# Graph-attention layer, one core: SyncE alone waits for the final stores, and shares the last block's first stores with GpSimd

## Chip, cores and metric

The kernel runs on one core of one Trainium2 chip. The metric is the device time of one execution in microseconds (us), lower is better. The kernel before takes 256.71 us, the median of 3 runs (256.52 to 256.77).

## What is computed

A graph-attention layer, then a residual and a layer norm, for N = 4096 nodes with D = 128 features. `adj` is a 4096 x 4096 matrix of int32 zeros and ones.

```python
s_i = emb @ attn[:d]
s_j = emb @ attn[d:]
e = leaky_relu(s_i + s_j.T, negative_slope=0.2)
e = e + where(adj > 0, 0.0, -1e9)
alpha = softmax(e, axis=1)
x = layernorm(x + alpha @ emb)
```

## The kernel before

The program is written engine by engine, and each engine runs its own list in the order in which it is written; semaphores are set by hand. SyncE (SP) and ScalarE (ACT) issue the loads: each takes one half of the partitions, in quadrants of 32 (`LOW_HALF` is quadrants 0 and 1 for SP, `HIGH_HALF` quadrants 2 and 3 for ACT). The matrix `adj` comes in 32 pieces, 8 blocks of 512 output rows with 4 pieces each. ScalarE makes mask bytes of a piece, VectorE (DVE) turns them and builds the weights (L721), and TensorE (PE) multiplies weights by features and sums in PSUM (L866, and L870 for the last block, where the four output tiles are summed one after the other).

Seven blocks are normalised by ScalarE and GpSimd (POOL) while the next block is computed, and GpSimd stores each with four DMAs (L346, semaphore `stored`). The last block of four tiles is finished in three groups, `FINAL_GROUPS`: tiles 0 and 1, then tile 2, then tile 3. `EARLY` is 1, so the first group is the early one:

- the early group (tiles 0 and 1): GpSimd computes scale and offset (L351 to L358), ScalarE applies them (L503) and raises `early_out_ready`, and GpSimd stores the group with four DMAs, one a quadrant, 32 KB each, whose completion counts on `early_stored`;
- the other two groups: VectorE normalises them (L698) and raises `last_out_ready`; SP stores quadrants 0 and 1, ACT quadrants 2 and 3, 16 KB each, two DMAs a group and engine, counted on `last_stored`.

All of these stores are issued by the one helper `store_last`, so each of them has line 279:

```python
queue.dma_start(out_v[f, q, :, k * D:(k + n) * D],
                x_raw[B * q:B * (q + 1), FINAL + v.start:FINAL + v.stop, :].rearrange("b k d -> b (k d)")
                ).then_inc(done, 16)
```

After its stores SP reads a flag, `again` (L306), that says whether a slow path for extreme inputs has to run; ACT, DVE and PE read it too (L526, L762, L911). With these inputs no engine takes that path. Then SP waits for `last_stored` (L316), which counts the stores of ACT too, and GpSimd waits for `early_stored` (L363). ACT waits for `stored` before it reads the flag (L522). At the end of the program's block (L91) each engine has a branch, a DRAIN and an event-semaphore instruction; GpSimd, which has two of these, gathers the arrivals of the others and then releases them. No engine leaves the block before all have come to its end. The waits on `last_stored` and `early_stored` are attached to the branches of L91.

Of the kernel before, what the change touches and what calls it, by code (L numbers as in the profile page):

```python
# [13 lines left out]
def gat_kernel(nc: bass.Bass, x: bass.AP, adj: bass.AP, attn: bass.AP, out: bass.AP):  # L14
# [11 lines left out]
    Q = 4  # L26
# [9 lines left out]
    LOW_HALF = (0, 1)  # L36
    HIGH_HALF = (2, 3)
# [23 lines left out]
    FINAL_GROUPS = [slice(0, 2), slice(2, 3), slice(3, 4)]  # L61
    EARLY = len(FINAL_GROUPS) - 2
# [28 lines left out]
    with ExitStack() as ctx:  # L91
# [3 lines left out]
        def sem(name):  # L95
            return ctx.enter_context(nc.semaphore(name))
# [111 lines left out]
        early_out_ready = sem("early_out_ready")  # L208
        last_out_ready = sem("last_out_ready")
        early_stored = sem("early_stored")  # L210
        last_stored = sem("last_stored")
# [37 lines left out]
        def load_x(queue, quadrants, part):  # L249

            first, stop = X_CUTS[part], X_CUTS[part + 1]
            for q in quadrants:
                queue.dma_start(x_raw[B * q:B * (q + 1), first:stop, :].rearrange("b (f k) d -> b f (k d)", k=K),  # L253
                                x_v[q, :, first // K:stop // K, :]).then_inc(x_loaded[part], 16)

        def load_piece(queue, quadrants, g):

            if g >= IN_FLIGHT:
                landed = g - IN_FLIGHT
                queue.wait_ge(adj_loaded[landed % ADJ_SLOTS], 16 * Q * (landed // ADJ_SLOTS + 1))  # L260
            if g == PROD_SLOT:
                queue.wait_ge(row_max_ready, 1)
            elif g == XT_SLOT:
                queue.wait_ge(s_i_in_psum, RB)
            elif ADJ_SLOTS <= g < ADJ_SLOTS + BY_DVE:
                queue.wait_ge(half_bytes_ready, 1)
                queue.wait_ge(first_bytes_ready, g - ADJ_SLOTS + 1)
            elif g >= ADJ_SLOTS + BY_DVE:
                queue.wait_ge(bytes_ready, g - ADJ_SLOTS - BY_DVE + 1)
            for q in quadrants:  # L270
                queue.dma_start(adj_in[B * q:B * (q + 1), g % ADJ_SLOTS, :, :, :],  # L271
                                adj_v[g // PIECES, g % PIECES, q, :, :, :, :]).then_inc(adj_loaded[g % ADJ_SLOTS], 16)

        def store_last(queue, g, q, done):

            v = FINAL_GROUPS[g]
            f, k = (FINAL + v.start) // K, v.start % K
            n = v.stop - v.start
# [3 lines that stand above are left out]
# [7 lines left out]
        @block.sync  # L289
        def _(sp):  # L290

            sp.dma_start(attn_row_in[:], attn[:, :].rearrange("d o -> o d")).then_inc(attn_loaded, 16)  # L292
            for part in range(X_PARTS):
                load_x(sp, LOW_HALF, part)
            for g in range(ALL_PIECES):
                load_piece(sp, LOW_HALF, g)


            for g in range(EARLY, len(FINAL_GROUPS)):
                sp.wait_ge(last_out_ready, g - EARLY + 1)  # L300
                for q in LOW_HALF:
                    store_last(sp, g, q, last_stored)


            sp.wait_ge(again_ready, 1)
            with sp.If(sp.value_load(again[0:1, 0:1], min_val=0, max_val=1) > 0):  # L306
                sp.wait_ge(stored, 16 * Q * NORM_GROUPS)
                sp.wait_ge(early_stored, 16 * Q * EARLY)
                sp.wait_ge(last_stored, 16 * Q * (len(FINAL_GROUPS) - EARLY))
                sp.dma_start(xi[:], xi_v).then_inc(inputs_again, 16)  # L310
                sp.dma_start(attn_col, attn[D:2 * D, :]).then_inc(inputs_again, 16)
                sp.dma_start(attn_row, attn[0:D, :].rearrange("d o -> o d").broadcast_to([P, D])).then_inc(inputs_again, 16)
                with sp.Fori(0, TILES) as t:
                    sp.wait_ge(adj_rows_free, t + 1)
                    sp.dma_start(adj_rows, adj[bass.ds(t * P, P), :]).then_inc(adj_rows_loaded, 16)
            sp.wait_ge(last_stored, 16 * Q * (len(FINAL_GROUPS) - EARLY))  # L316

        @block.gpsimd
        def _(pool):
            nc.gpsimd.memset(ident[:], 0.0).then_inc(ident_zeroed, 1)  # L320
            pool.wait_ge(ident_zeroed, 1)
            nc.gpsimd.affine_select(out=ident[:], in_=ident[:], compare_op=ALU.not_equal, fill=1.0, base=0,
                                    pattern=[[-1, P]], channel_multiplier=1).then_inc(consts_ready, 1)
            nc.gpsimd.memset(half[:], -0.5)
            nc.gpsimd.memset(eps[:], EPS)
            nc.gpsimd.memset(rden[:], 0.0)
            nc.gpsimd.memset(worst[:], 0.0).then_inc(worst_ready, 1)
            pool.wait_ge(products_ready, STRIPES)
            nc.gpsimd.tensor_scalar(neg_last[:], x_raw[:, :, DEN], -1.0, 0.0, ALU.mult, ALU.add).then_inc(neg_last_ready, 1)
            pool.wait_ge(neg_last_ready, 1)  # L330
            pool.wait_ge(factors_ready, 1)
            nc.gpsimd.tensor_tensor(last_x[:], neg_last[:], d_j[:], ALU.mult).then_inc(last_x_ready, 1)

            for g in range(NORM_GROUPS):

                pool.wait_ge(total_ready, g + 1)
                nc.gpsimd.tensor_scalar(neg_mean[:, 0:K], total[:, 0:K], -1.0 / D, 0.0, ALU.mult, ALU.add).then_inc(mean_ready, 1)  # L337
                pool.wait_ge(squares_ready, g + 1)
                nc.gpsimd.tensor_scalar(variance[:, 0:K], square_sum[:, 0:K], 1.0 / D, EPS, ALU.mult, ALU.add).then_inc(variance_ready, 1)
                pool.wait_ge(variance_ready, g + 1)  # L340
                nc.gpsimd.tensor_tensor(rstd[:, 0:K], variance[:, 0:K], half[:, 0:K], ALU.pow).then_inc(rstd_ready, 1)  # L341
                pool.wait_ge(rstd_ready, g + 1)
                nc.gpsimd.tensor_tensor(offset[:, 0:K], neg_mean[:, 0:K], rstd[:, 0:K], ALU.mult).then_inc(offset_ready, 1)  # L343
                pool.wait_ge(out_ready, g + 1)
                for q in range(Q):
                    pool.dma_start(out_v[g, q, :, :],  # L346
                                   x_raw[B * q:B * (q + 1), g * K:(g + 1) * K, :].rearrange("b k d -> b (k d)")).then_inc(stored, 16)

            for g, v in enumerate(FINAL_GROUPS[:EARLY]):
                pool.wait_ge(moments_ready, v.stop)  # L350
                nc.gpsimd.tensor_scalar(variance[:, v], moments[:, v, 1], 1.0, EPS,  # L351
                                        ALU.mult, ALU.add)
                nc.gpsimd.tensor_scalar(neg_mean[:, v], moments[:, v, 0], -1.0, 0.0,
                                        ALU.mult, ALU.add).then_inc(variance_ready, 1)
                pool.wait_ge(variance_ready, NORM_GROUPS + g + 1)
                nc.gpsimd.tensor_tensor(rstd[:, v], variance[:, v], half[:, v], ALU.pow).then_inc(rstd_ready, 1)
                pool.wait_ge(rstd_ready, NORM_GROUPS + g + 1)
                nc.gpsimd.tensor_tensor(offset[:, v], neg_mean[:, v], rstd[:, v], ALU.mult).then_inc(offset_ready, 1)  # L358
            for g in range(EARLY):
                pool.wait_ge(early_out_ready, g + 1)  # L360
                for q in range(Q):
                    store_last(pool, g, q, early_stored)
            pool.wait_ge(early_stored, 16 * Q * EARLY)  # L363

        @block.scalar
        def _(act):
# [608 lines left out]
```

## Time and profile before

| what | value |
|---|---|
| median of 3 runs (lowest to highest) | 256.71 us (256.52 to 256.77) |
| the profiled execution's own time | 257.18 us |
| its span, first to last instruction | 255.3 us |
| PE busy | 242.9 us, 95% of the span |
| DVE busy | 233.6 us, 91% |
| ACT busy | 175.4 us, 69% |
| POOL busy | 36.5 us, 14% |
| DMA traffic | 71.51 MB |

Times in the rows are us from the span's start unless marked ns. "Busy" counts work instructions alone; branches, drains, semaphore instructions and the issuing of DMAs by SP and ACT are not in it, and are found under the line that holds them, with a q behind the engine's name (POOLq is GpSimd's sequencer). "DMA to landing" runs from the start of an issue to the moment at which its data have landed.

### The profile page before, as it was taken

The page shows a single profiled execution, that of the slowest core. Times are in us where ns is not written, and L with a number is a line of the kernel's source. Part 1 is how long each engine was busy: PE and PEld are TensorE (multiplying, and loading weights), DVE is VectorE, ACT ScalarE, POOL GpSimd, SP SyncE. Part 2 cuts the span into 40 slices and gives each one's busy share as a digit, 9 for nine tenths or more (in the row PEclk, how much of TensorE's full clock was granted, in tenths as well). Part 3 has the DMA queues.
Part 4 walks back from the last instruction along what each step waited for, and adds up shares of the span by engine and source line. Part 5 has one row for each costly group of instructions (what it writes and reads, how often), then busy time and mean ns, then how long its engine had stood idle before and what let it go on. Part 6 is the DMA issues. An engine that isn't in the chain of part 4 may idle for free.

```text
span 255.3 us, 2776 instructions
## 1 busy us (share of the span) xinstructions
PE 242.9 (95%) x801; PEld 127.9 (50%) x801; DVE 233.6 (91%) x383; ACT 175.4 (69%) x257; POOL 36.5 (14%) x76
## 2 busy tenths in 40 slices
PE   7998989989999999999999999999999999999980
PEld 6743434434444444444444444444444444899970
DVE  1979899989999999999999999999999999999552
ACT  0589999998499669495986579578965579204410
POOL 1000000000052003300430003300320004303322
PEclk9999999999999999999999999999999999999997
DMA  7999999999999999999999999999999940100101
GB/s 199 309 347 348 348 349 347 349 342 348 347 328 360 349 348 348 348 335 348 348 347 364 347 348 348 353 349 348 349 360 350 346 116 0 45 0 4 41 0 45
DMA packets 70227, 71.51 MB, mean 280 GB/s; under 512 B 2881, under 2 KB 68674, under 8 KB 70210
## 3 DMA queue, kind: packets, MB, share of 16 engines
q10 hardware_dynamic: 34592, 34.67, 43.5%
q1 hardware_dynamic: 34594, 34.67, 43.4%
q0 software_dynamic: 1024, 1.97, 2.5%
q8 instruction: 7, 0.11, 0.2%
q14 instruction: 10, 0.08, 0.1%
HBM read 69.21 MB, written 2.10 MB: 279 GB/s over the span
## 4 chain that ended last, share of the span: by engine, by line
PE 81%; ACT 6%; DMA 5%; issue 2%; ACTq 2%; SPq 1%; POOL 1%; DVE 1%
PE psum L866 69%; PE psum L870 11%; DMA adj_in<-in_adj_dram 5%; ACT xj L400 2%; ACTq L271 2%; ACT mask_bytes L412 2%; ACT mask_bytes L418 1%; PE psum L862 1%; SPq L253 1%; POOL out_dram L279 1%; ACT x_raw L503 0%; SPq L271 0%; DVE weights L721 0%; DVE x_raw L666 0%; SPq L292 0%
## 5 line engine op out<-in xcount | busy, mean ns | idle before, releaser
L866 PE MATMUL psum<-weights,xj 128*128 128x512 f32 x448 | 194.5, 593 | 2.9 <-ACT xj L400 2.0
L721 DVE SCALAR_TENSOR_TENSOR weights<-q_row,r_j,mask_t 128x512 f32<-128x512 f32 x256 | 172.2, 740 | 0.3
L866 PEld LDWEIGHTS psum<-weights,xj 128*128 128x128 f32 x448 | 84.0, 190 | 109.2 <-issue 82.2
L418 ACT ACTIVATE mask_bytes<-adj_in 128x4096 uint8<-128x4096 int32 x27 | 97.3, 3613 | 22.7 <-DMA adj_in<-in_adj_dram 15.2
L607 DVE STREAM_TRANSPOSE mask_t<-mask_bytes 128x1024 uint32<-128x1024 uint32 x27 | 33.4, 1236 | 0.9 <-ACT mask_bytes L418 0.9
L870 PEld LDWEIGHTS psum<-xj,weights 128*128 128x128 f32 x256 | 28.8, 192 | 0.5 <-issue 0.5
L870 PE MATMUL psum<-xj,weights 128*128 128x128 f32 x256 | 28.9, 275 | 0.0
L337 POOL TENSOR_SCALAR neg_mean<-total 128x4 f32<-128x4 f32 x7 | 1.6, 223 | 158.4 <-ACT x_raw L431 158.4
L431 ACT ACTIVATE x_raw<-x_raw 128x128 f32<-128x128 f32 x28 | 8.2, 295 | 15.3 <-DVE x_raw L666 15.3
L346 POOL DMA_DIRECT2D out_dram<-x_raw x28 | 14.6, 525 | 19.3 <-ACT x_raw L445 19.3
L412 ACT ACTIVATE mask_bytes<-adj_in 128x2048 uint8<-128x2048 int32 x9 | 17.0, 1901 | 0.0
L400 ACT ACTIVATE xj<-x_raw,last_x,d_j 128x127 f32<-128x127 f32 x32 | 13.2, 485 | 1.2 <-issue 1.2
L445 ACT ACTIVATE x_raw<-x_raw,offset,rstd 128x128 f32<-128x128 f32 x28 | 11.5, 480 | 2.6 <-POOL offset L343 2.6
L438 ACT ACTIVATE unused<-x_raw,neg_mean 128x128 f32<-128x128 f32 x28 | 10.9, 390 | 2.5 <-POOL neg_mean L337 2.5
L426 ACT COPY sums<-psum 128x512 f32<-128x512 f32 x7 | 4.1, 585 | 12.2 <-PE psum L866 12.2
L341 POOL TENSOR_TENSOR rstd<-variance,half 128x4 f32<-128x4 f32 x7 | 9.9, 1419 | 0.6
L666 DVE SCALAR_TENSOR_TENSOR x_raw<-psum,rden,x_raw 128x127 f32<-128x127 f32 x32 | 9.2, 343 | 0.4
L620 DVE STREAM_TRANSPOSE mask_t<-mask_bytes 128x512 uint32<-128x512 uint32 x10 | 7.1, 708 | 1.8 <-ACT mask_bytes L412 1.6
L833 PE MATMUL psum<-adj_in,attn_iw 128*128 128x512 f32 x16 | 7.6, 598 | 0.0
L511 ACT ACTIVATE deviations<-moments,eps 128x1 f32<-128x1 f32 x2 | 0.6, 294 | 8.5 <-DVE moments L690 8.5
L654 DVE TENSOR_SCALAR rden<-psum 128x4 f32<-128x4 f32 (+2 forms) x10 | 1.5, 154 | 5.3 <-PE psum L870 5.3
L822 PE MATMUL psum<-ident,x_raw 128*128 128x128 f32 x32 | 6.0, 350 | 0.3 <-DMA x_raw<-in_x_dram 0.3
(65 smaller groups left out, 81.7 us busy)
## 6 DMA issues: line engine op xcount, KB each, us to landing
adj_in<-in_adj_dram ACTq DMA_DIRECT2D x64, 512.0 KB, 13.0
adj_in<-in_adj_dram SPq DMA_DIRECT2D x64, 512.0 KB, 13.6
out_dram<-x_raw POOLq DMA_DIRECT2D x28, 64.0 KB, 5.3
x_raw<-in_x_dram ACTq DMA_DIRECT2D x4, 128.0 KB, 3.2
x_raw<-in_x_dram SPq DMA_DIRECT2D x4, 128.0 KB, 3.5
x_raw<-in_x_dram ACTq DMA_DIRECT2D x2, 256.0 KB, 6.1
x_raw<-in_x_dram SPq DMA_DIRECT2D x2, 256.0 KB, 7.0
out_dram<-x_raw POOLq DMA_DIRECT2D x4, 32.0 KB, 1.8
```

The lines of the kernel that those rows point to most:

```text
L341: nc.gpsimd.tensor_tensor(rstd[:, 0:K], variance[:, 0:K], half[:, 0:K], ALU.pow).then_inc(rstd_ready, 1)
L346: pool.dma_start(out_v[g, q, :, :], x_raw[B * q:B * (q + 1), g * K:(g + 1) * K, :].rearrange("b k d -> b (k d)")).then_inc(stored, 16)
L400: nc.scalar.activation(xj[:, c, 0:DEN], x_raw[:, c, 0:DEN], ACT.Identity, bias=last_x[:, c:c + 1], scale=d_j[:, c:c + 1]).then_inc(xj_scal ...
L412: half_bytes = nc.scalar.activation(mask_bytes[:, g % BYTE_SLOTS, :, :, part], adj_in[:, g % ADJ_SLOTS, :, :, part], ACT.Sign)
L418: nc.scalar.activation(mask_bytes[:, g % BYTE_SLOTS, :, :, :], adj_in[:, g % ADJ_SLOTS, :, :, :], ACT.Sign).then_inc(bytes_ready, 1)
L438: last = nc.scalar.activation(unused[:, k, :], tile(g * K + k), ACT.Square, bias=neg_mean[:, k:k + 1], accum_out=square_sum[:, k:k + 1])
L445: last = nc.scalar.activation(tile(g * K + k), tile(g * K + k), ACT.Identity, bias=offset[:, k:k + 1], scale=rstd[:, k:k + 1])
L607: nc.vector.transpose(dst.rearrange("p f (r a) -> p r f a", a=B), src).then_inc(mask_ready, 1)
L666: nc.vector.scalar_tensor_tensor(features, sums_of(n, t)[:, 0:DEN], rden[:, t:t + 1], features, ALU.mult, ALU.add).then_inc(y_ready, 1)
L721: nc.vector.scalar_tensor_tensor(weights[:, slot_of(n, c), :], q_row[:, n * BANK:(n + 1) * BANK], r_j[:, c:c + 1], mask_t[:, (n * PIECES + ...
L866: nc.tensor.matmul(banks[SUM_BANK[n % 2]][:, :], xj[:, c, :], weights[:, slot_of(n, c), :], start=(c == 0), stop=(c == CHUNKS - 1)).then_i ...
L870: return nc.tensor.matmul(banks[((BLOCKS - 1) * K + t) % 8][:, 0:D], weights[:, slot_of(BLOCKS - 1, c), t * P:(t + 1) * P], xj[:, c, :], s ...
```

## The change

SP issues quadrants 0 and 1 of the early group, ahead of its other four stores, and counts them on `last_stored`. GpSimd issues quadrants 2 and 3 of it, still on `early_stored`, and no longer waits for them; SP waits for both semaphores at the end. The counts in the waits are adapted. The slow path's waits change with them and are not executed.

```diff
@@ sync (SP)
+            for g in range(EARLY):
+                sp.wait_ge(early_out_ready, g + 1)
+                for q in LOW_HALF:
+                    store_last(sp, g, q, last_stored)
             for g in range(EARLY, len(FINAL_GROUPS)):
                 sp.wait_ge(last_out_ready, g - EARLY + 1)
                 for q in LOW_HALF:
...
                 sp.wait_ge(stored, 16 * Q * NORM_GROUPS)
-                sp.wait_ge(early_stored, 16 * Q * EARLY)
-                sp.wait_ge(last_stored, 16 * Q * (len(FINAL_GROUPS) - EARLY))
+                sp.wait_ge(early_stored, 16 * len(HIGH_HALF) * EARLY)
+                sp.wait_ge(last_stored, 16 * (Q * len(FINAL_GROUPS) - len(HIGH_HALF) * EARLY))
...
-            sp.wait_ge(last_stored, 16 * Q * (len(FINAL_GROUPS) - EARLY))
+            sp.wait_ge(early_stored, 16 * len(HIGH_HALF) * EARLY)
+            sp.wait_ge(last_stored, 16 * (Q * len(FINAL_GROUPS) - len(HIGH_HALF) * EARLY))
 
         @block.gpsimd
...
             for g in range(EARLY):
                 pool.wait_ge(early_out_ready, g + 1)
-                for q in range(Q):
+                for q in HIGH_HALF:
                     store_last(pool, g, q, early_stored)
-            pool.wait_ge(early_stored, 16 * Q * EARLY)
```

On GpSimd the end of the list reads so before (a row is a line, an operation, its output and input, and in brackets the semaphores that it waits for):

```order
L358 TENSOR_TENSOR offset<-neg_mean,rstd 128x2 [waits rstd_ready]
L279 DMA out_dram<-x_raw 32x256 [waits early_out_ready]
L279 DMA out_dram<-x_raw 32x256 x3
L91 UNCONDITIONAL_BRANCH [waits early_stored]
```

and so after the change (its line 363 is line 358 of before):

```order
L363 TENSOR_TENSOR offset<-neg_mean,rstd 128x2 [waits rstd_ready]
L279 DMA out_dram<-x_raw 32x256 [waits early_out_ready]
L279 DMA out_dram<-x_raw 32x256
L91 UNCONDITIONAL_BRANCH
```

Two of four DMA issues are gone from GpSimd, and the branch to the block's end waits for nothing. On SP, between its last loads of `adj` and the reading of the flag, the difference is:

```order
 L271 DMA adj_in<-in_adj_dram 32x16x256
+L279 DMA out_dram<-x_raw 32x256 [waits early_out_ready]
+L279 DMA out_dram<-x_raw 32x256
 L279 DMA out_dram<-x_raw 32x128 [waits last_out_ready]
 L279 DMA out_dram<-x_raw 32x128
 L279 DMA out_dram<-x_raw 32x128 [waits last_out_ready]
 L279 DMA out_dram<-x_raw 32x128
```

The two stores of the early group stand ahead of SP's four others. The branch of L91 on SP now waits for two semaphores:

```order
-L91 UNCONDITIONAL_BRANCH [waits last_stored]
...
+L91 UNCONDITIONAL_BRANCH [waits last_stored,early_stored]
```

Nothing moves on PE, DVE and ACT.

## Rows read from the trace of the kernel before

**Rows 1.** The page: the span, and busy time by engine.
```profile
span 255.3 us, 2776 instructions
PE 242.9 (95%) x801; PEld 127.9 (50%) x801; DVE 233.6 (91%) x383; ACT 175.4 (69%) x257; POOL 36.5 (14%) x76
```

**Rows 2.** End of the chain that ended last: start us, us, what.
```profile
225.38 20.56 PE psum L870 x184
...
247.64 0.78 ACT x_raw L503 x2
248.42 0.28 issue
248.70 0.59 POOL out_dram L279
249.29 0.00 issue
249.29 1.47 POOL out_dram L279 x3
```

**Rows 3.** The block's end, L91, on all engines: ns min/median/max, first and last start us.
```profile
L91 POOLq EVENT_SEMAPHORE  x2: 17/17/17, 255.1 to 255.2; - x2
L91 DVEq DRAIN  x1: 17/17/17, 251.7 to 251.7; - x1
L91 PEldq DRAIN  x1: 73/73/73, 251.9 to 251.9; - x1
L91 POOLq COMPARE_BRANCH  x1: 33/33/33, 252.3 to 252.3; - x1
L91 POOLq DRAIN  x1: 2674/2674/2674, 252.4 to 252.4; - x1
L91 ACTq DRAIN  x1: 81/81/81, 252.7 to 252.7; - x1
L91 SPq COMPARE_BRANCH  x1: 38/38/38, 253.1 to 253.1; - x1
L91 SPq DRAIN  x1: 7/7/7, 253.2 to 253.2; - x1
```

**Rows 4.** What SP's queue waited for, 247 to 256 us: total, times, longest.
```profile
SPq L91 <- PEq L91: 2.0, 1, 2.0
SPq L91 <- DMA out_dram<-x_raw: 0.9, 1, 0.9
```

**Rows 5.** The program's start, L965: GpSimd's DRAIN.
```profile
L965 POOLq DRAIN  x1: 169/169/169, 0.3 to 0.3; - x1
```

**Rows 6.** GpSimd's stores of the early group (L279), the first two, then the last two.
```profile
L279 POOL DMA_DIRECT2D out_dram<-x_raw x2: 496/544/593, 248.7 to 249.3; - x2
DMA to landing us min/median/max: 1.8/1.8/1.8
L279 POOL DMA_DIRECT2D out_dram<-x_raw x2: 496/498/501, 249.8 to 250.3; - x2
DMA to landing us min/median/max: 1.9/1.9/2.0
```

**Rows 7.** The last two stores of SP, and of ACT (L279).
```profile
L279 SPq DMA_DIRECT2D out_dram<-x_raw x2: 423/428/432, 250.3 to 250.8; - x2
DMA to landing us min/median/max: 1.9/2.0/2.0
L279 ACTq DMA_DIRECT2D out_dram<-x_raw x2: 438/440/443, 250.4 to 250.9; - x2
DMA to landing us min/median/max: 2.1/2.2/2.2
```

**Rows 8.** Timeline from 248 us: start us, us, engine, line, instructions.
```profile
249.12 0.34 DVE L698 TENSOR_SCALAR x_raw<-x_raw,moments,rstd 128x128 f32<-128x128 f32 x1
249.49 1.75 SPq L279 DMA_DIRECT2D out_dram<-x_raw  x4
249.49 1.81 ACTq L279 DMA_DIRECT2D out_dram<-x_raw  x4
```

**Rows 9.** Issues on SP: other loads, and the branch of the flag (L306).
```profile
L253 SPq DMA_DIRECT2D x_raw<-in_x_dram x6: 353/427/432, 1.1 to 3.4; - x6
L271 SPq DMA_DIRECT2D adj_in<-in_adj_dram x64: 579/2816/6242, 3.9 to 193.4; - x64
L306 SPq COMPARE_BRANCH  x1: 50/50/50, 252.1 to 252.1; - x1
```

**Rows 10.** Instruction queues by DMA window: 252 to 252.7, then 253.1 to 253.6.
```profile
q8 instruction: 1, 0.02, 11.5%
q14 instruction: 1, 0.01, 5.7%
```

## Prediction
> **What bounds the kernel now.** I read the page first: TensorE is busy for 95% of the span [rows 1]. The change touches none of its work, so all that it can win or lose lies behind the last product. The second view is the chain of waits [rows 2]. TensorE's sum of tile 2 ends at 245.94, ScalarE finishes the early group at 248.42, and then the chain runs over GpSimd's four store issues, 248.70 to 250.76. There it stops, 4.5 us before the span ends at 255.3, because the rest is sequencer instructions that are not counted as work. So the third view is the block's end, L91, engine by engine [rows 3]. In order of arrival: VectorE drains at 251.7, TensorE at 251.9, ScalarE at 252.7, SP at 253.2. GpSimd branches at 252.3, starts its DRAIN at 252.4 and is in it for 2674 ns, until 255.04. Its two event-semaphore instructions (gather, release) follow at 255.1 and 255.2, and the span ends at 255.3, 0.26 us behind the drain's end. Every other engine has stood ready since 253.2: SP waited 2.0 us for the release, after 0.9 us for the last store to land [rows 4]. The row names TensorE as releaser, but TensorE had arrived at 251.9; the release comes from GpSimd. **The end of the kernel is GpSimd's DRAIN, and that starts where the last of GpSimd's four stores has landed.** The landing that the wait of L363 waits for: the last issue starts at 250.27 and lands 2.0 us later, 252.27 [rows 6], and the branch goes at 252.3.
>
> **The change, part by part.**
>
> Removed: GpSimd's wait. The branch then follows the last issue at once instead of at its landing. With four issues that would be 250.77 instead of 252.3, so 1.5 us.
>
> Removed: two of GpSimd's issues, the last two, 496 to 501 ns each [rows 6], so 1.0 us more. GpSimd's issues then end at 249.29 + 0.50 = 249.79. The step from its release to the start of the drain was 0.1 us (252.3 to 252.4), so the drain starts at about 249.9, 2.5 us earlier.
>
> The drain's length with two stores in flight is shown by no row, since both drains of the trace find the queue empty. The bounds are 169 ns, the drain of the start, before GpSimd has stored anything [rows 5], and 2674 ns plus all the time until its stores have landed. I take 2674 ns flat: it is the one drain at the same place behind the same kind of DMA. Then it ends at 249.9 + 2.67 = 252.6. With 169 ns it would end at 250.1; for the span the two are the same, since both lie before SP's 253.2. GpSimd's gather is then complete only when SP arrives.
>
> Added on SP: two issues in front of its four. Its queue has been idle since the loads. `early_out_ready` comes at 248.42; SP follows a release by 0.03 us (VectorE ends at 249.46, SP issues at 249.49 [rows 8]). Two issues at the 0.43 us of SP's later stores [rows 7] end at 249.31, which is 0.18 us before the moment at which SP has its next work, so they cost nothing. The cover is thin: SP's issues of the larger loads of `x` take 353 to 432 ns, but those of `adj` at least 579 ns [rows 9]. With 579 ns the two end at 249.61 and all that SP has behind them slips by 0.12 us. Who waits for SP? Only the block's end.
>
> Moved wait: SP waits for `early_stored` as well. GpSimd's second issue starts at 249.29 and lands 1.8 us later, at 251.1 [rows 6]; SP's own two, issued before 249.0, land by about 251. SP itself reaches its branch of the flag at 252.1 [rows 9] and then waits for ACT's last store, which is issued at 251.30 - 0.44 = 250.86 and lands 2.2 us later, at 253.06 [rows 7, 8]. So the new wait ends 2 us before the old one: free. If SP's stores slip by 0.12 us, its last one lands at 250.81 + 0.12 + 2.0 = 252.9, still before ACT's.
>
> Traffic: before, the last two GpSimd stores (249.8 to 252.3) flew beside the 16 KB stores of SP and ACT; now that data leaves earlier. ACT's last two stores took 2.1 and 2.2 us, SP's 1.9 and 2.0, GpSimd's first 1.8 [rows 6, 7]. At best ACT's last takes 1.8 and lands at 252.7, 0.4 us earlier; at worst nothing changes. I take nothing, and keep the 0.4 for the range.
>
> **The sum.** SP's drain is over at 253.2, as before. A step of about 0.1 us from SP's arrival to GpSimd, which until now had no place on the path (my estimate, from the 0.1 us between landing and branch and between branch and drain in rows 3), then the 0.26 us of gather and release: the span ends at 253.55 instead of 255.3, so 1.75 us less. The profiled execution takes 257.18 us by its own clock, 0.47 over the median of the runs; its 1.88 us outside the span I leave as they are. 257.18 - 1.75 = 255.43 for a profiled execution, and against the runs 256.71 - 1.75 = **255.0 us**. What is late next is ACT's last store. Removing the wait alone would have given a drain end of 250.77 + 0.1 + 2.67 = 253.54 and a gain of 1.5 us; the moved stores are thus worth some 0.25 us, as they bring the drain's end below SP's arrival.
>
> **The rivals.**
>
> *The drain waits for GpSimd's own stores (A').* If stores in flight count as GpSimd's work, the drain cannot be done before they land at 251.1. If its 2.67 us then begin, it ends at 251.1 + 0.1 + 2.67 = 253.9, the span at 254.15, 1.15 us less: 255.6 us. For it: the 2.67 us stand behind DMAs while the drain of the start took 0.17. Against it: 2.67 us were needed although everything had landed, so the time is no waiting for data. The Trainium skill's "PSUM — Partial Sum Buffer", section "Engine vs sequencer instructions", says that a drain waits for the engine to go fully idle; it does not say whether a transfer in flight counts as activity. By that rule, read strictly, the result is this rival's; no row before shows it.
>
> *The instruction queues.* One block of instructions is fetched between 252 and 252.7, another between 253.1 and 253.6 [rows 10], while everybody stands in the barrier. If an engine needs one of them to leave, a release at 253.4 comes too early, and the end (in the span or behind it) is at about 253.9 instead of 253.55: 255.4 us. For it: the fetch begins behind the end of all work. Against it: at 255.3 the engines left within 0.1 us, which says only that the block was there by then.
>
> *The change does not do what it says.* The drain might end by something that the change leaves alone, for example 1.95 us behind the landing of the last store of any engine (253.06 + 1.98 = 255.04). Then it only gets longer by as much as it starts earlier, 5.1 us, and the time stays at 256.7. For it: only one long drain is seen, so its start may be coincidence. Against it: the other engines' drains beside stores in flight or just landed took 7 and 81 ns [rows 3].
>
> *Slower: the drain pays for each open store.* If the drain, in addition to its 2.67 us, works 2.67 us on every store that it finds open, it takes 3 x 2.67 = 8.0 us from 249.9, ends at 257.9, and the span at 258.2: 2.9 us more, 259.6 us. It decides from a drain of 5.1 us on (249.9 + 5.1 = 255.04); above 5.7 us the loss could be measured. For it speaks that the change starts a drain with open stores for the first time; against it, that the drain before had 32 stores behind it and took 2.67 us in all, 84 ns for each.
>
> **How the numbers follow.** My forecast, the flat drain off the path: 0.55, at 255.0, by itself 254.6 (ACT's landing 0.4 earlier) to 255.2 (SP's slip and the 0.13 us by which the runs scatter). Instruction fetch: 0.12, at 255.4. Drain behind the landing: 0.18, at 255.6. No effect: 0.10, at 256.7. Slower: 0.05, at 259.6. A measurement of this kernel can tell 0.2%, 0.5 us, from no change. The first three cases all lie more than that below 256.71, so faster is 0.85, the same 0.10, slower 0.05. The range has to take in the first three; from 254.5, a tenth below the forecast's own low end, to 256.0, a third of a microsecond above the drain behind the landing, for a drain that is a little longer there. Left out are the 0.15 of the last two cases.
>
> **What would show it.** Right: in the rows of the block's end GpSimd's branch stands at 249.8 and its DRAIN starts at 249.9 and ends before 253; SP's DRAIN stays at 253.2 and the span ends within 0.4 us of it; SP's queue no longer waits 2 us for a release; SP's six stores are issued without a gap that moves the last one past 250.8. The drain's length tells the cases apart: 2.67 us or less is mine, 4.0 is the drain behind the landing, 5.1 the unchanged end, more than 5.7 the loss. A span of 253.9 with a drain that ended at 252.6 speaks for the instruction queues. The prediction is wrong if the drain still ends last, or if ACT's last store lands later than 253.1.

## Result: 2.3 us faster, more than forecast

The changed kernel takes **254.08 us**, the median of 4 runs (253.61 to 254.91), against 256.74 us for 4 runs of the kernel before (256.52 to 256.91). The ratio is 0.991, 95% interval 0.9891 to 0.9928, so it is faster by 1.8 to 2.8 us, 2.3 us by the ratio; the two medians themselves lie 2.66 us apart. The forecast was 255.0 us in a range of 254.5 to 256.0: the direction is right, the time lies below the range.

The profiled execution of the changed kernel took 254.91 us, of which the span is 253.0. Its page, for [rows 1]:

```profile
span 253.0 us, 2776 instructions
PE 243.4 (96%) x801; PEld 128.1 (51%) x801; DVE 233.6 (92%) x383; ACT 175.5 (69%) x257; POOL 36.4 (14%) x74
```

TensorE's and VectorE's work is the same to 0.5 us; GpSimd has two instructions fewer. The block's end, for [rows 3], with L310 in place of L306 for SP's branch of the flag:

```profile
L91 POOLq EVENT_SEMAPHORE  x2: 17/17/17, 252.8 to 252.9; - x2
L91 POOLq DRAIN  x1: 3249/3249/3249, 249.0 to 249.0; - x1
...
L91 SPq COMPARE_BRANCH  x1: 38/38/38, 252.6 to 252.6; - x1
L91 ACTq DRAIN  x1: 81/81/81, 252.6 to 252.6; - x1
L91 SPq DRAIN  x1: 7/7/7, 252.8 to 252.8; - x1
...
L310 SPq COMPARE_BRANCH  x1: 50/50/50, 252.1 to 252.1; - x1
```

GpSimd's DRAIN is now recorded from 249.0 on, while its first store is still being issued (the second follows from 249.2 to 249.7), and is over at 252.3. SP arrives at 252.8 and is the last; 0.2 us later the span ends. The waits of SP's queue, for [rows 4] (L321 is the wait for `last_stored`):

```profile
SPq L321 <- DMA out_dram<-x_raw: 0.3, 1, 0.3
...
SPq L91 <- PEq L91: 0.2, 1, 0.2
```

The 2.0 us in which SP stood at the barrier are 0.2. The timeline, for [rows 8], and the last two stores of SP and ACT with their landing, for [rows 7]:

```profile
247.46 0.86 ACT L507 ACTIVATE x_raw<-x_raw,offset,rstd 128x128 f32<-128x128 f32 x2
248.35 2.87 SPq L279 DMA_DIRECT2D out_dram<-x_raw  x6
248.62 1.09 POOL L279 DMA_DIRECT2D out_dram<-x_raw  x2 [1.30 <-ACT x_raw L507]
249.42 1.82 ACTq L279 DMA_DIRECT2D out_dram<-x_raw  x4
```

```profile
L279 SPq DMA_DIRECT2D out_dram<-x_raw x2: 421/467/513, 250.2 to 250.8; - x2
DMA to landing us min/median/max: 1.6/1.7/1.7
L279 ACTq DMA_DIRECT2D out_dram<-x_raw x2: 443/450/457, 250.3 to 250.8; - x2
DMA to landing us min/median/max: 1.5/1.7/1.8
```

SP's six issues end at 251.22, practically where four ended before (251.24). But ACT's last store, issued at 250.8, lands 1.5 us later, where it took 2.2 before [rows 7]. The last landing is now that of SP's own last store, 1.7 us behind its issue; it comes 0.47 us earlier than the last landing of before, both counted from the end of ScalarE's work on the early group. That is what the forecast had left out.

**A ruler for what follows.** Executions of one kernel differ by more than the runs shown before had led me to think: 255.89 to 257.53 us for 17 runs of the kernel before, beside the first four experiments, and 256.04 to 258.10 for 23 beside the next four. In the profiles the difference stands ahead of the change. ScalarE finishes the early group at 248.41 in the profile of before and at 248.33 in that of the change, but at 247.1 to 248.4 over all profiles of this study; already VectorE's first weights start anywhere from 18.4 to 19.7 us. So I measure the **tail**: from the moment at which ScalarE has normalised the early group (the end of L503, L507 in the changed kernel) to the end of the span, from the nanoseconds of the records. It is 6.90 us before and 4.67 after, 2.23 us less.

| kernel | median, us | ratio to before | tail, us | GpSimd's drain ends | SP's drain ends |
|---|---|---|---|---|---|
| before | 256.74 | | 6.90 | 6.67 | 4.85 |
| the change | 254.08 | 0.991 (0.9891 to 0.9928) | 4.67 | 3.95 | 4.46 |
| e1, the change again | 254.23 | 0.9913 (0.9895 to 0.9931) | 4.69 | 3.95 | 4.47 |
| e2, wait moved only | 254.88 | 0.994 (0.9923 to 0.9957) | 5.41 | 5.18 | 5.10 |
| e3, stores moved only | 255.05 | 0.9943 (0.9926 to 0.9961) | 5.58 | 5.35 | 4.41 |
| e4, four on SP | 256.16 | 0.999 (0.9975 to 1.0006) | 6.78 | 1.36 | 6.56 |
| e5, block stores on SP | 254.92 | 0.9938 (0.9915 to 0.9961) | 4.87 | 4.62 | 4.66 |
| e6, before + early drain | 254.75 | 0.9927 (0.9902 to 0.9951) | 5.07 | 4.60 | 4.85 |
| e7, split by columns | 255.92 | 0.9978 (0.9965 to 0.9991) | 6.42 | 6.19 | 4.48 |
| e8, split by rows | 255.87 | 0.9985 (0.9963 to 1.0006) | 6.43 | 6.20 | 4.51 |
| e9, one each + drain | 253.85 | 0.9911 (0.9896 to 0.9925) | 4.70 | 4.24 | 4.49 |
| e10, one each | 255.20 | 0.995 (0.9936 to 0.9964) | 5.62 | 5.38 | 4.49 |
| e11, three on SP | 254.07 | 0.9912 (0.9895 to 0.9928) | 4.79 | 3.40 | 4.58 |
| e12, the change + drain | 254.08 | 0.9913 (0.9899 to 0.9926) | 4.74 | 2.80 | 4.52 |

The last two columns are us into the tail. The median of e11 is that of its five fast runs; a sixth was slow (262.21 us, granted clock 0.945 against 0.988 to 0.998). Each ratio is to the kernel before on the same chip (256.29 us beside e1 to e4, 256.46 beside e5 to e8, 256.41 beside e9 to e12). In every row the tail ends 0.2 us behind the later of the two drains.

### The profile page after: what moved, and what is told of

Same layout as the page of the kernel before. It is cut to its first block, busy times and chain, and to the rows that moved or that the text cites. A ratio compares the mean times of both kernels' runs of the same rounds, so it can differ in the third digit from the quotient of the medians.

```text
span 253.0 us, 2776 instructions
## 1 busy us (share of the span) xinstructions
PE 243.4 (96%) x801; PEld 128.1 (51%) x801; DVE 233.6 (92%) x383; ACT 175.5 (69%) x257; POOL 36.4 (14%) x74
## 4 chain that ended last, share of the span: by engine, by line
PE 87%; ACT 6%; ACTq 2%; DVE 2%; issue 2%; POOL 0%; POOLq 0%; DVEq 0%
PE psum L870 70%; PE psum L874 11%; ACT mask_bytes L416 2%; ACTq L271 2%; PE psum L826 2%; ACT xj L404 2%; ACT mask_bytes L422 1%; PE psum L811 1%; PE psum L866 1%; PE psum L837 1%; ACT adj_in L386 1%; DVE weights L725 1%; PE psum L814 0%; ACT adj_in L377 0%; PE psum L853 0%
## 5 line engine op out<-in xcount | busy, mean ns | idle before, releaser
L346 POOL TENSOR_TENSOR rstd<-variance,half 128x4 f32<-128x4 f32 x7 | 10.0, 1423 | 0.6
L837 PE MATMUL psum<-adj_in,attn_iw 128*128 128x512 f32 x16 | 8.3, 641 | 0.0
L377 ACT COPY adj_in<-psum 128x512 f32<-128x512 f32 x8 | 4.5, 583 | 3.8 <-PE psum L826 3.8
## 6 DMA issues: line engine op xcount, KB each, us to landing
x_raw<-in_x_dram ACTq DMA_DIRECT2D x2, 256.0 KB, 6.2
x_raw<-in_x_dram SPq DMA_DIRECT2D x2, 256.0 KB, 7.1
```

Source lines behind the costliest of these rows:

```text
L837: nc.tensor.matmul(banks[bank][:, :], attn_iw[:], xT[:, rb * BANK:(rb + 1) * BANK], start=True, stop=True).then_inc(s_i_in_psum, 1)
```

## Experiments

### The two halves of the change

**e1** is the changed kernel, unaltered.

> The changed kernel a second time, unaltered. The question is the 0.45 us by which the last stores of SP and ACT landed sooner than before (1.5 to 1.9 us from issue against 1.9 to 2.2), and the spread of its four times, 253.61 to 254.91. Theory 'traffic': the landing is shorter because GpSimd's last two stores are no longer under way beside them; then this profile shows 1.5 to 1.9 us again and the time is near 254.1. Rival 'chance': landing times differ from execution to execution; then this profile may show 2.0 to 2.2 us and a span near 253.4.

Its SP and ACT stores took 1.48 to 1.91 us to land, store by store within 0.03 us of the first profile, and its tail is 4.69 us. The shorter landing is no chance of one execution. **e2** moves only the wait:

```diff
             for g in range(EARLY):
                 pool.wait_ge(early_out_ready, g + 1)
                 for q in range(Q):
                     store_last(pool, g, q, early_stored)
-            pool.wait_ge(early_stored, 16 * Q * EARLY)
```

with `sp.wait_ge(early_stored, 16 * Q * EARLY)` at SP's end.

> GpSimd issues all four early stores as before, but SP waits for them. Theory 'flat drain of 2.6 us counted from the end of GpSimd's last issue': that issue ends at 250.7, the drain at 253.3, the span at 253.55, and the time is 1.7 us under the kernel before, about 255.0. Under 'traffic' SP's and ACT's last stores land 1.9 to 2.2 us after issue again, so SP arrives at 253.2. Rival 'the drain has to see GpSimd's stores land, then takes 1.2 us' (the changed kernel's 251.06 to 252.29): landing 252.2, drain end 253.4, which the profile tells apart by the time from landing to the drain's end, 1.1 us here or 1.2; it is told better by the next kernel.

**e3** is the change with GpSimd's wait put back:

```diff
                 for q in HIGH_HALF:
                     store_last(pool, g, q, early_stored)
+            pool.wait_ge(early_stored, 16 * len(HIGH_HALF) * EARLY)
```

> SP issues two of the early stores as in the change, but GpSimd still waits for its own two before the block's end. Flat drain: GpSimd's branch at 251.1, drain 251.2 to 253.8 (2.6 us), span 254.1, time about 255.3 to 255.6, some 1.1 to 1.3 us under before. Rival 'drain ends 1.2 us behind the landing': drain 251.2 to 252.3, no loss against the change, time near 254.1.

The drains, e2 first, then e3:

```profile
L91 POOLq DRAIN  x1: 3605/3605/3605, 249.1 to 249.1; - x1
```

```profile
L91 POOLq COMPARE_BRANCH  x1: 33/33/33, 250.9 to 250.9; - x1
L91 POOLq DRAIN  x1: 2511/2511/2511, 251.0 to 251.0; - x1
```

e2's tail is 5.41 us, 1.49 less than before; e3's 5.58, 1.32 less. Both halves help alone, and together they give 2.23, less than the sum, since SP then ends the kernel. e3 refutes a drain that is over 1.2 us behind the landing: it takes 2.51 us although both stores have landed. By the medians e3 is 1.24 us under before, as expected, and e2 1.41 where 1.7 was expected: its drain ended 2.81 us behind the last issue instead of 2.6. e2 ends last on GpSimd by 0.08 us only. ACT's last store, with all four early stores on GpSimd, needs the long landing again:

```profile
L279 ACTq DMA_DIRECT2D out_dram<-x_raw x2: 433/438/443, 249.5 to 250.0; - x2
DMA to landing us min/median/max: 2.1/2.3/2.4
```

**e4** leaves GpSimd no store in the last block: `for q in range(Q)` on SP, GpSimd's loop removed.

> SP issues all four early stores, GpSimd none; its last stores are those of the block before, at 238 to 240 us, long landed. Flat drain: it starts at 247.4 and still takes 2.6 us (ends at 250.0). Rival 'the drain waits for something of stores just issued': it takes 0.2 us or little more. Rival 'cost for each store of the program' (2674 ns for 32, 84 ns each): 28 stores, 2.34 us. The span is SP's business: eight issues of 0.43 us in a row push its last one from 250.8 to about 251.4, its flag read to 252.7, its last landing to 253.1, so the time is 0.3 to 0.6 us above the changed kernel's.

```profile
L91 POOLq DRAIN  x1: 2606/2606/2606, 246.7 to 246.7; - x1
```

GpSimd's last instruction ends at 246.98, the drain at 249.35: 2.37 us, although the last of GpSimd's 28 stores was issued seven microseconds before. That is nearly 28 x 84 ns (2.35 us), and speaks for a cost for each store and against a flat one. But the time is 2 us above the change, not 0.3 to 0.6. Below, under e11, is why.

### What the drain costs

**e5**: the kernel before, with its 28 block stores issued by SP, four behind each of four loads and the rest behind the last load:

```diff
...
             for g in range(ALL_PIECES):
                 load_piece(sp, LOW_HALF, g)
+                if g - 10 in TAKE_SUMS_AT:
+                    store_block(TAKE_SUMS_AT.index(g - 10))
+            for g in range(4, NORM_GROUPS):
+                store_block(g)
```

`store_block(g)` waits for `out_ready` and issues the four DMAs of L346 on SP; GpSimd's own are taken out.

> The kernel before with its wait on GpSimd, but the 28 stores of the first seven blocks are issued by SP (behind loads that leave them time); GpSimd issues only the four early stores. Theory 'the drain costs 84 ns for each store that GpSimd has issued in the program' (2.33 us for 28, 2.51 for 30, 2.67 for 32 so far): drain 4 x 84 ns = 0.33 us, GpSimd through before SP arrives, the wait on GpSimd costs nothing, time 1.7 to 2.0 us under before, if the loads do not suffer from the stores on SP's queue. Rival 'flat cost as soon as GpSimd has stored anything': drain 2.5 to 2.7 us, no gain.

**e6**: the kernel before with one line more:

```diff
+            nc.gpsimd.drain()
             for g, v in enumerate(FINAL_GROUPS[:EARLY]):
                 pool.wait_ge(moments_ready, v.stop)
```

> The kernel before plus one DRAIN on GpSimd behind the last store of block 7, at 240.3, where GpSimd idles until 245.8. Theory, cost for each store since the last drain: the early one takes 28 x 84 ns = 2.35 us under cover, the last one 4 x 84 ns = 0.33 us; the span ends with SP, time 1.7 to 2.0 us under before. Rival, cost for each store of the whole program, paid at each drain: the last one takes 2.67 us again, no gain.

The final drain of e5, then the two of e6 (the early one has line 349):

```profile
L91 POOLq DRAIN  x1: 387/387/387, 251.5 to 251.5; - x1
```

```profile
L91 POOLq DRAIN  x1: 381/381/381, 252.6 to 252.6; - x1
...
L349 POOLq DRAIN  x1: 3343/3343/3343, 239.6 to 239.6; - x1
```

Four stores since the last drain, or in the whole program: 0.39 us in e5, 0.38 in e6. The early drain of e6 runs from 239.6 to 242.9, under cover, and one line brings the kernel before from 256.46 to 254.75 us although GpSimd still waits for its four stores. The flat cost is refuted, and so is a cost for all stores of the program at each drain. e5's tail is 2.04 us shorter than that of before, but its time only 1.54 us, less than the 1.7 to 2.0 expected: its executions have 2.1 to 2.2 us outside the span, where those of before have 1.8. Why is open.

**e7** and **e8** double the number of stores in the changed kernel, by columns and by rows (e8 shown):

```diff
                 for q in range(Q):
-                    pool.dma_start(out_v[g, q, :, :], ...
+                    for h in range(0, B, 16):
+                        pool.dma_start(out_v[g, q, h:h + 16, :], ...
```

> The changed kernel, but each of the 28 block stores of GpSimd is cut in two by columns (32 rows of 1 KB each instead of 2 KB), so 58 stores in all. 84 ns for each store: 4.87 us from the end of the last issue, the drain ends 2.3 us later than in the changed kernel, last of all, and the time is 1.8 to 2.0 us above it, about 256.1. Flat cost: 2.5 us, no difference, 254.1.

> The same, cut in two by rows (16 rows of 2 KB each), 58 stores in all but the same number of rows as before. If the cost is for each store: 4.87 us as in e7. If it is for each row moved (2.6 ns for each of 32 x 30 rows): 2.5 us and the time of the changed kernel, 254.1.

```profile
L91 POOLq DRAIN  x1: 5487/5487/5487, 248.1 to 248.1; - x1
```

```profile
L91 POOLq DRAIN  x1: 5499/5499/5499, 248.4 to 248.4; - x1
```

Counted from the end of GpSimd's last issue (248.76 and 249.05) these are 4.81 us in both, for 58 stores of either shape: the cost is for each DMA, not for each row. The times, 255.92 and 255.87 us, are near the 256.1 expected. Together: 0.38 us for 4 stores, 2.37 for 28, 2.51 for 30, 2.67 for 32, 4.81 for 58. The slope between 4 and 32 is (2674 - 384) / 28 = **82 ns for each store since the drain before**, with 0.06 us on top. Where the last stores are still open when the drain begins, the time behind the last issue is up to 0.2 us above this line: 2.56 us for 28 (the early drain of e6), 2.52 for 29 (e11), 2.57 for 30 (the change), 2.81 and 2.82 for 32 (e2, e10). The line is not shown below 4 stores; the drain of the start, with none, took 0.17 us [rows 5].

### Stores behind an instruction fetch

**e11** gives SP three early stores (`for q in (0, 1, 2)`) and GpSimd one.

> SP issues three of the early stores, GpSimd one. e4 with four had a last store that took 3.18 us to land, where the one before it took 1.49: it was issued at 3.20 us of the tail and a 16 KB packet of instructions (queue 8, 1.2 us long) went out at 4.09, just before its data. Theory 'store behind the instruction fetch': with seven stores the last one is issued at 2.8 and its packets are out by 4.0, so it lands in 1.5 to 1.7 us at 4.3 to 4.5, and the tail is 4.8 to 4.9 us, 0.2 above the changed kernel. Rival 'each store on SP beyond six costs more': tail above 5.5 us.

The last store of SP: of e4, the one before it, then it; and of e11:

```profile
L279 SPq DMA_DIRECT2D out_dram<-x_raw x2: 419/420/421, 250.3 to 250.7; - x2
DMA to landing us min/median/max: 1.5/1.5/1.5
L279 SPq DMA_DIRECT2D out_dram<-x_raw x1: 421/421/421, 251.2 to 251.2; - x1
DMA to landing us min/median/max: 3.2/3.2/3.2
```

```profile
L279 SPq DMA_DIRECT2D out_dram<-x_raw x1: 422/422/422, 250.6 to 250.6; - x1
DMA to landing us min/median/max: 1.5/1.5/1.5
```

And what the DMA engines carried in e4, from 252.0 to 252.6, then from 253.0 to 253.4:

```profile
q8 instruction: 1, 0.02, 12.4%
q1 hardware_dynamic: 45, 0.02, 10.8%
```

```profile
q1 hardware_dynamic: 3, 0.00, 2.9%
```

The eighth store's data start at 252.1; a 16 KB packet of instructions began at 252.08 and lasts 1.19 us. Of the store's 48 packets 45 are out by 252.35, but the last three go from 253.24 on, just as that packet ends. With seven stores on SP nothing collides, and the tail is 4.79 us, as expected. A store of 16 KB that comes 0.4 us later costs 2 us. That the packet and the three stragglers share one DMA engine is inferred from their times; the records don't tell the engine. That an eighth store on SP is slow for some other reason is not excluded by a run of its own.

### An attempt at a faster version

**e9** has the early drain and hands one store of tile 2 (from SP) and one of tile 3 (from ACT) to GpSimd, **e10** the same without the drain, **e12** the change with the drain alone:

```diff
                 for q in HIGH_HALF:
                     store_last(pool, g, q, early_stored)
+            pool.wait_ge(last_out_ready, 1)
+            store_last(pool, EARLY, LOW_HALF[1], early_stored)
+            pool.wait_ge(last_out_ready, 2)
+            store_last(pool, EARLY + 1, HIGH_HALF[1], early_stored)
...
```

The loops of SP and ACT leave out these two, and the counts in SP's waits follow.

> An attempt at a faster version. The changed kernel, plus the early DRAIN behind block 7, plus GpSimd takes one store of tile 2 from SP and one of tile 3 from ACT, so that SP issues five and ACT three. Counted from the end of ScalarE's normalisation of the early group (the tail of before is 6.90 us, of the changed kernel 4.67): GpSimd issues its fourth store by 2.5 us, its drain takes 0.06 + 4 x 0.082 = 0.39 us and is over by 2.9; the last stores of SP and ACT are issued 0.43 us earlier and land at 3.8 to 3.9 (with GpSimd's store beside them perhaps 4.2); ACT's flag read ends 0.44 us earlier, at 3.95. Tail 4.2 to 4.4 us, 0.3 to 0.5 us under the changed kernel. Rival 'traffic eats it': GpSimd's late stores cost the others what they cost in before (landings of 2.1 to 2.4 us), the last lands at 4.3 and the tail stays at 4.6.

> The same without the early DRAIN. GpSimd then has 32 stores to account for at the end: 2.5 + 0.06 + 32 x 0.082 = 5.2 us, the tail is 5.3 to 5.4 us, GpSimd is the last again, 0.6 to 0.7 us above the changed kernel. If the tail is as in e9, the cost for each store is wrong.

> The control for e9: the changed kernel with the early DRAIN alone. GpSimd's last drain shrinks from 2.5 us (30 stores) to 0.06 + 2 x 0.082 = 0.22 us behind its last issue and ends at 1.6 us of the tail instead of 3.95. SP arrives at 4.46 in either, so the tail stays at 4.67 and the time does not change. If the time falls, the drain still cost something in the changed kernel.

The drains, e9, e10, e12:

```profile
L91 POOLq DRAIN  x1: 2187/2187/2187, 249.1 to 249.1; - x1
```

```profile
L91 POOLq DRAIN  x1: 3341/3341/3341, 249.9 to 249.9; - x1
```

```profile
L91 POOLq DRAIN  x1: 2077/2077/2077, 248.9 to 248.9; - x1
```

e10 is 0.95 us of tail worse than the change (0.6 to 0.7 were expected), since its drain counts 32 stores after a late last issue and ends 2.82 us behind it. e9 wins nothing: 4.70 us. SP's last store was issued 0.3 us earlier, but took 2.1 us to land beside GpSimd's, which took 2.0:

```profile
L279 SPq DMA_DIRECT2D out_dram<-x_raw x1: 428/428/428, 249.2 to 249.2; - x1
DMA to landing us min/median/max: 2.1/2.1/2.1
```

The rival "traffic eats it" holds. And both drains behind the early one are longer than their count: e12's should have ended 0.22 us behind the last issue, at 1.6 us of the tail, and ends at 2.80; e9's at 3.0 and ends at 4.24. GpSimd's last store lands at 2.67 in e12 and at 4.03 in e9, so the drains end 0.12 and 0.21 us behind the landing. From GpSimd's last issue to its landing, e9, then the two of e12:

```profile
L279 POOL DMA_DIRECT2D out_dram<-x_raw x1: 496/496/496, 249.1 to 249.1; - x1
DMA to landing us min/median/max: 2.0/2.0/2.0
```

```profile
L279 POOL DMA_DIRECT2D out_dram<-x_raw x2: 498/546/593, 248.5 to 249.1; - x2
DMA to landing us min/median/max: 1.8/1.8/1.8
```

**The drain does wait for GpSimd's own stores**: that is read from these two coincidences, 1.4 us apart, and no run moved the landing alone. In the changed kernel the count (30 stores) runs from the last issue on and lasts until 3.95, longer than the landing at 2.68, and hides that. e12's time, 254.08 us, confirms that the drain is off the path after the change. No version here beats the change beyond the intervals.

## Why the prediction was right and where it failed

- **What bounds the end.** Right: GpSimd's DRAIN was last, and with the wait and two issues gone it is not. SP is last, in both profiles of the change.
- **"I take 2674 ns flat."** The value was nearly right, the reason wrong, and that is luck. Behind the last issue the drain took 2.57 us, within 0.1 of the forecast's 2.67, because 30 stores cost nearly what 32 do. The 84 ns for each store stood in the prediction only as an argument against the slower rival; it is what the runs show. With 58 stores (e7, e8) the drain is the last again, at 6.2 us of the tail, and the forecast that SP decides would have been wrong.
- **The drain starts at 249.9, after the last issue.** It is recorded from 249.0 on, during the issues, and holds the wait for them. For the end that made no difference.
- **"Traffic: I take nothing."** This is the step that failed: a term of the sum put at nothing, which measured 0.39 us. With all four early stores on GpSimd the last landing of the kernel stands at 4.67 us of the tail (4.84 in e2, 4.67 in e6, 4.48 in e5), with two at 4.20 (4.16 to 4.27 in e1, e3, e7, e8 and e12). ACT's last store shows it most: 2.2 to 2.4 us (2.0 in e5) against 1.5 (1.8 in e8). Where GpSimd has one early store, or none, all other SP and ACT stores take 1.5 to 1.6 (e11, e4, but for the one in e4 behind the fetch). It is the queue more than the moment at which the data leave: SP's third store of e11 is issued at 0.88 us of the tail and GpSimd's second of the change at 0.89, both 32 KB, yet ACT's first store, issued at 1.09 in both, takes 1.53 us in e11 and 1.91 in the change. How GpSimd's stores lengthen the others is open.
- **"So the new wait ends 2 us before the old one: free."** Not quite. The wait for a second semaphore is an instruction of its own on SP (L321 above): with it SP's drain ends 0.26 us behind the last landing (the change, e1, e2, e9, e12), without it 0.18 (before, e4, e5, e6). So the landing is 0.47 us earlier and SP's arrival 0.39: at 4.46 us of the tail instead of 4.85, the 0.4 that I had kept for the range only.
- **The release.** I had put 0.1 us for SP's arrival at GpSimd and 0.26 for the release; measured from SP's drain to the end it is 0.21. Another 0.15 us. (Even before, the drain ended at 255.08 and not at 255.04, so gather and release took 0.23.) By the records the forecast's sum is 6.90 - 4.85 - 0.36 = 1.69 us (1.75 in its rounded numbers); with these two it is 1.69 + 0.39 + 0.15 = 2.23 us, which is what was measured.
- **The cost of SP's two issues.** Right: they were through at 0.84 us of the tail, and the next began at 1.09, where it had begun before (1.08). SP's last issue came 0.07 us later than before, because one of 513 ns stood in the row.
- **The range.** Applied to the median of before shown at the first, the measured tail gives 256.71 - 2.23 = 254.5, the edge of the range. The remaining 0.4 us no step of the kernel explains. It lies within what executions scatter: the medians of the change and of before differ by 2.06 us beside e1 and by 2.66 here. I had put 0.13 us for the scatter, from three runs; four of the changed kernel spread over 1.3 us, 17 and 23 of the kernel before over 1.6 and 2.1. A forecast with the right terms would have stood at the edge of the range, and on which side of it the median fell was chance.
- **Rivals.** Drain behind the landing: half true, as e9 and e12 show, but it did not decide here. No effect: not seen. A drain that gets dearer for open stores: by 0.14 us, not by 2.67 for each; e2's drain, begun with stores open, ended 2.81 us behind the last issue, where 32 landed stores cost 2.67 before. Instruction queues at the barrier: refuted. In the profile of the change the two fetches begin at 252.41 and 253.25, and the first lasts until 253.28, yet the span ends at 252.99, and the time outside it is 1.9 us as before. The queues from 252.4 to 252.9, then from 252.9 to 253.4:

```profile
q8 instruction: 1, 0.02, 10.9%
```

```profile
q14 instruction: 1, 0.01, 6.6%
```

- **Slips of the prediction.** The first fetch before ran from 252.54 to 253.83, while ACT and SP were still on their way to the barrier (252.7 and 253.2), not "while everybody stands in the barrier". By its own numbers that rival's time is 256.71 - (255.3 - 253.9) = 255.3 us, not 255.4, and the 1.95 us behind the last landing is 1.98 in its own sum. None of these moves the forecast.

## What to carry to other kernels

Where a kernel ends in GpSimd's DRAIN, count the DMAs that GpSimd has issued: each costs 82 ns there. Start that drain early by letting another engine wait for the landings, or put a `drain` into an idle gap of GpSimd before the end; one such line took 1.83 us off the tail of the kernel before, where this change took 2.23 (e6). Then look at the last landing: in these runs stores on GpSimd's queue lengthened those of the two others, and a store that slipped behind an instruction fetch cost more than any of the issues that were saved.

## What was not expected of the hardware

- A DRAIN on GpSimd behind 4 to 58 DMAs took 0.06 us plus 82 ns for each DMA that GpSimd had issued since its last drain, up to 0.2 us more where they were still open, whatever the DMA's shape, and in no run did it end before the last of them had landed (0.12 us behind it in e12, the closest). The Trainium skill's "PSUM — Partial Sum Buffer", section "Engine vs sequencer instructions", says that a drain waits for the engine to go fully idle; e12 and e9 agree, with GpSimd's own transfers counted as activity.
- A 16 KB store took 1.5 to 1.6 us to land where SP and ACT stored alone (e4, but for the one behind the fetch), 1.5 to 1.9 in the change with two early stores on GpSimd, and up to 2.4 with four (e2).
- One 16 KB packet of instructions, 1.19 us long, stood beside a store whose landing took 3.18 us, where the store before it took 1.49 (e4); that the one held up the other is inferred from their times.
